# Interaction tower of 16 batches on one core: the last four batches' dense layers in groups of 2 and 2, and GpSimd makes part of batch 14's second products

## What is computed

```python
def _L0_rec_ref(x, Ws, bs):            # x (2048, 16, 256)
    xk = x
    outs = []
    for i in range(3):
        z = jnp.einsum('bfe,bge->bfge', x, xk).reshape(B_, F_ * F_, E_)
        z = jnp.swapaxes(z, 1, 2)
        z = jnp.einsum('bcl,oc->bol', z, Ws[i]) + bs[i][None, :, None]
        z = jax.nn.relu(z)
        z = jnp.sum(z, axis=-1)
        outs.append(z)
        xk = jnp.broadcast_to(z[:, :, None], (B_, F_, E_))
    return jnp.concatenate(outs, axis=1)
e = jnp.stack([tbl_0[ids[:, 0]], ..., tbl_15[ids[:, 15]]], axis=1)
z = _L0_rec_ref(e, L0_rec_Ws, L0_rec_bs)
h = jnp.concatenate([z.reshape(2048, -1), dense_ctx], axis=1)
h = jnp.maximum(h @ W_top1 + b_top1, 0.0)      # 64 -> 512
h = jnp.maximum(h @ W_top2 + b_top2, 0.0)      # 512 -> 256
y = h @ W_top3                                 # 256 -> 1
```

## Time and profile before

| | us |
|---|---|
| runs | 576.73, 579.08, 579.23 |
| median | 579.08 |
| the profiled execution | 579.74 |
| its span | 578.0 |
| last recorded instruction ends | 576.47 |

### The profile page before, as it was taken

How to read it: one execution, slowest core, us unless ns; L and a number is a source line. 1 busy time by engine, 2 the same in 40 slices (tenths; PEclk the granted TensorE clock), 3 DMA queues, 4 the chain that set the end, 5 groups by cost and what they waited for, 6 DMA issues and landing times.

```text
span 578.0 us, 10773 instructions
## 1 busy us (share of the span) xinstructions
PE 476.3 (82%) x3990; PEld 190.8 (33%) x3990; DVE 542.8 (94%) x326; ACT 498.7 (86%) x1471; POOL 467.8 (81%) x354
## 2 busy tenths in 40 slices
PE   5559888687888798878989788798869888789988
PEld 5213233232333333232333323233333323233324
DVE  1697999999999999999999999999999999999994
ACT  1143698999999999999999999989999999999875
POOL 6665888889888888888888889888888888888630
PEclk9689898999989989998999999799999989999979
DMA  3352212221222122212221222212212212210000
GB/s 98 92 145 74 75 56 57 63 64 56 74 58 64 56 71 72 67 56 74 62 64 56 69 60 61 73 57 82 64 56 66 61 60 74 57 54 1 1 2 0
DMA packets 14334, 35.43 MB, mean 61 GB/s; under 512 B 5493, under 2 KB 5879, under 8 KB 14266
## 3 DMA queue, kind: packets, MB, share of 16 engines
q0 software_dynamic: 12288, 33.57, 20.3%
q1 hardware_dynamic: 1994, 1.17, 0.8%
HBM read 34.71 MB, written 0.01 MB: 60 GB/s over the span
## 4 chain that ended last, share of the span: by engine, by line
DVE 38%; ACT 28%; PE 18%; issue 10%; POOL 3%; another core or an unknown queue 1%; DMA 1%; ACTq 0%; DVEq 0%; POOLq 0%
DVE prod L436 32%; ACT outer L637 15%; PE z_ps L827 8%; DVE outer L485 6%; ACT outer L627 3%; ACT sq L582 3%; POOL x_rows L342 3%; PE t_ps L790 3%; ACT relu L593 2%; ACT xt L574 2%; PE turn_ps L898 1%; PE turn_ps L902 1%; PE turn_ps L860 1%; PE zs_ps L842 1%
## 5 line engine op out<-in xcount | busy, mean ns | idle before, releaser
L436 DVE TENSOR_TENSOR prod<-t_ps,xt 128x2048 f32<-128x2048 f32 x190 | 420.8, 2281 | 11.0 <-remote 6.7
L342 POOL DMA_INDIRECT x_rows<-in_tbl,ids_sb x256 | 248.4, 970 | 73.1 <-issue 62.0
L637 ACT ACTIVATE outer<-outer,bias_sb 128x256 f32<-128x256 f32 x476 | 236.7, 518 | 3.0 <-DVE outer L485 3.0
L827 PE MATMUL z_ps<-prod,w_sb 128*32 128x512 f32 x1520 | 191.2, 622 | 37.3 <-DVE prod L436 34.3
L356 POOL TENSOR_TENSOR intra<-xt 128x1024 f32<-128x1024 f32 (+4 forms) x90 | 205.1, 2281 | 6.0 <-PE z_ps L827 4.5
L574 ACT ACTIVATE xt<-t_ps 128x512 f32<-128x512 f32 x128 | 75.2, 604 | 45.2 <-PE t_ps L790 21.7
L637 ACT ACTIVATION_READ_ACCUMULATOR outer<-outer,bias_sb 128x1 f32 x476 | 100.2, 210 | 0.0
L485 DVE TENSOR_TENSOR outer<-y_ps,z_all 128x1408 f32<-128x1408 f32 (+2 forms) x60 | 93.4, 1598 | 4.5 <-ACT outer L627 3.5
L790 PE MATMUL t_ps<-ident,x_rows 128*128 128x128 f32 x512 | 81.2, 288 | 19.0 <-DMA x_rows<-in_tbl,ids_sb 7.1
L827 PEld LDWEIGHTS z_ps<-prod,w_sb 128*32 128x32 f32 x1520 | 45.8, 111 | 124.8 <-issue 93.3
L790 PEld LDWEIGHTS t_ps<-ident,x_rows 128*128 128x128 f32 x512 | 55.9, 143 | 81.8 <-issue 59.6
(11 more groups left out here) (69 smaller groups left out, 219.1 us busy)
## 6 DMA issues: line engine op xcount, KB each, us to landing
x_rows<-in_tbl,ids_sb POOLq DMA_INDIRECT x256
w_sb<-in_w SPq DMA_DIRECT2D x1, 512.0 KB
feat<-in_dense SPq DMA_DIRECT2D x1, 128.0 KB
w_sb<-in_w SPq DMA_DIRECT2D x1, 128.0 KB
ids_sb<-in_ids SPq DMA_DIRECT2D x1, 120.0 KB
ident<-in_identity SPq DMA_DIRECT2D x1, 64.0 KB, 2.1
w_sb<-in_w0t SPq DMA_DIRECT2D x1, 64.0 KB
sel_sb<-in_sel SPq DMA_DIRECT2D x1, 48.0 KB
```

Of the source, the lines that this page charges most:

```text
L342: pool.indirect_dma_start(out=x_rows[:, par, f, :], out_offset=None, in_=tables[f], in_offset=bass.IndirectOffsetOnAxis(ap=ids_sb[:, NF * ...
L436: dve.tensor_tensor(prod[:, m % PROD_RING, half, :].rearrange("p (f g s) -> p f g s", f=QF, g=QF), t_ps[:, tbank(b, q, half), :, :].unsque ...
L637: act.activation(outer_of(b)[:, o // OP, o % OP, :], outer_of(b)[:, o // OP, o % OP, :], ACT.Relu, bias=bias12_sb[:, layer - 1, o:o + 1], ...
L827: mm = pe.matmul(z_ps[j * GR:(j + 1) * GR, m % 2, 0:n], w0_sb[:, half, slot, :], src[:, half, j * n:(j + 1) * n], start=(slot == 0 and hal ...
```

## The change

The dense groups of the tail become two and two batches (256 columns each). The first group's features, batches 12 and 13, are ready early, so TensorE runs its first layer directly behind z of layer 0 and the y step of group 2. For this the steps of group 2 move up: h2 step 0 goes to frame 14's slot `mlp_c`, h2 step 1 to frame 15's `mlp_a`, y to `mlp_b`. ScalarE's order in the tail changes with it, and batch 14's features are turned only behind the first dense group, directly ahead of batch 15's in TensorE's program; the 8 warming transposes stand ahead of both. `VECTOR_SUMS` gives VectorE 12 channels of batch 15's layer 1 and ScalarE 4. GpSimd makes channels 12 to 15 of batch 14's layer 2 (`outer_former`) from a new copy of y on ScalarE (`copy_y_former`), and VectorE's second piece shrinks from 8 channels to 4.

```diff
-LAST_TURN = ((0, "feat"), (0, "mlp_a"), (0, "yt"), (0, "mlp_b"), (1, "feat"), (0, "mlp_c"), (2, "feat"))
+LAST_TURN = ((0, "feat"), (0, "mlp_a"), (0, "yt"), (0, "mlp_b"), (1, "feat"), (2, "feat"))
...
-TAIL_GROUPS = (3, 1)
+TAIL_GROUPS = (2, 2)
...
-VECTOR_SUMS = {(2, 2): 4, (1, 1): 10, (1, 2): 8}
+VECTOR_SUMS = {(2, 2): 4, (1, 1): 12, (1, 2): 8}
...
         def mlp_slot(frame, kind):
...
+            if frame == LAST or (frame, kind) == (LAST - 1, "mlp_c"):
+                i = M1 + (frame - LAST + 1) * (1 + s)
+                return (t, i, range(M2 if i == M1 + M2 else M1)) if i <= M1 + M2 else None
...
+            def outer_former():
+
+                pool.wait_ge(y_copied, 1)
+                pool.wait_ge(z_ready, z_count(LAST - 1, 1))
+                o = NF - LAST_OP
+                y = y_former[:, :, :, :].rearrange("p f c o -> p o (f c)")
+                pool.tensor_tensor(
+                    outer[:, o // OP, o % OP:o % OP + LAST_OP, :].rearrange("p o (g f) -> p o g f", g=NF),
+                    y.unsqueeze(2).to_broadcast([P, LAST_OP, NF, NF]),
+                    z_all[:, (LAST - 1) % 2, 1, :].unsqueeze(1).unsqueeze(3).to_broadcast([P, LAST_OP, NF, NF]),
+                    ALU.mult).then_inc(pool_outer, 1)
...
-                n = op(b)
+                n = min(op(b), vector_channels(b, layer) - o)
...
+            def copy_y_former():
+
+                act.wait_ge(y_turned, LAST)
+                act.activation(y_former[:, :, :, :], y_ps[:, :, :, 1, NF - LAST_OP:NF], ACT.Copy).then_inc(y_copied, 1)
...
                 if i == 0:
-                    pe.wait_ge(turn_moved, turn(LAST + 1 + g, "feat") + 1)
+                    pe.wait_ge(turn_moved, turn(LAST + 2 * g, "feat") + 1)
+                if g == 0 and i == 2:
+                    pe.wait_ge(outer_done, piece(LAST - 1, 2, OP) + 1)
```

More of the change, by code:

```diff
@@ L37 @@
 FIRST_READ = (1, 0)
-WARM = {"first": 28, "second": 22, "end": 8}
+WARM = {"first": 28, "second": 22, "tail": 8}
 PROD_RING = 3
@@ L86, in build @@
         z_all = sb("z_all", [P, 2, NL, NF])
+        y_former = sb("y_former", [P, QF, GROUPS, LAST_OP])
         y_last = sb("y_last", [P, QF, GROUPS, 2, LAST_OP])
@@ L212, in op, with vector_channels @@
             return LAST_OP if b == LAST else OP
-        def vector_channels(b):
-            return NF - LAST_OP if b == LAST else NF
+        def vector_channels(b, layer):
+            return NF - LAST_OP if (b, layer) > (LAST - 1, 1) else NF
         def piece(b, layer, o):
-            return 2 * PIECES * b + vector_channels(b) // op(b) * (layer - 1) + o // op(b)
+            return 2 * PIECES * b + vector_channels(b, 1) // op(b) * (layer - 1) + o // op(b)
         def mlp_slot(frame, kind):
@@ L228, in mlp_slot @@
             if kind == "mlp_c":
-                done = t if frame == LAST else t - 1
-                return (done, M1 + M2, range(M2)) if done >= 0 and (at == 0 or frame == LAST) else None
+                return (t - 1, M1 + M2, range(M2)) if t > 0 and at == 0 else None
             if at < 2:
                 return t, 2 * at + s, range(1)
-            if frame == LAST:
-                return t, M1 + s, range(M1)
             return t, M1 + at - 2, range(M1 // 2 * s, M1 // 2 * (s + 1))
@@ L419, in _ @@
             multiply_last_unit(1)
+            outer_former()
             outer_last(1)
@@ L478, in outer_piece @@
                         dve.wait_ge(y_turned, b + 1)
-                        if b == LAST:
-                            dve.wait_ge(y_copied, 1)
+                        if b >= LAST - 1:
+                            dve.wait_ge(y_copied, b - LAST + 2)
                     if (b, layer) != (LAST, 1):
@@ L491, in outer_pieces @@
             def outer_pieces(b, layer):
-                for o in range(0, vector_channels(b), op(b)):
+                for o in range(0, vector_channels(b, layer), op(b)):
                     outer_piece(b, layer, o)
@@ L498, in vector_sum @@
                 for o in range(first, last):
-                    if o < vector_channels(b):
+                    if o < vector_channels(b, layer):
                         dve.wait_ge(outer_done, piece(b, layer, o) + 1)
                     else:
-                        dve.wait_ge(pool_outer, layer)
+                        dve.wait_ge(pool_outer, 1 if b < LAST else 1 + layer)
                     dve.scalar_tensor_tensor(
@@ L548, in _ @@
             outer_pieces(LAST, 1)
-            vector_sum(LAST, 1, 6, 16)
+            vector_sum(LAST, 1, 4, 16)
             outer_pieces(LAST, 2)
@@ L731, in _ @@
             copy_tile(LAST, 3, 1)
+            copy_y_former()
             move_z0(LAST - 1)
@@ L751, in _ @@
             sum_outer(LAST - 1, 2, 4, 8)
[L752 removed]
             mlp_in(LAST, "mlp_b")
[L754 to L757, removed]
+            sum_outer(LAST, 1, 0, 4)
             tail_move(0, 0)
@@ L761, in _ @@
             tail_move(0, 3)
-            mlp_in(LAST, "mlp_c")
-            sum_outer(LAST, 2, 0, 2)
-            sum_outer(LAST, 2, 2, 4)
+            sum_outer(LAST - 1, 2, 8, 12)
             tail_move(0, 4)
             tail_move(0, 5)
-            sum_outer(LAST, 2, 4, 6)
-            sum_outer(LAST, 2, 6, 8)
+            move_feat(LAST - 1)
+            sum_outer(LAST, 2, 0, 4)
+            sum_outer(LAST, 2, 4, 8)
             move_feat(LAST)
@@ L949, in keep_warm @@
             def keep_warm(when):
-                out = turn_ps[:, 0:P] if when == "end" else zs_ps[:, 0:P]
                 for _ in range(WARM[when]):
-                    pe.transpose(out, ident[:, :], ident[:, :])
+                    pe.transpose(turn_ps[:, 0:P] if when == "tail" else zs_ps[:, 0:P], ident[:, :], ident[:, :])
             pe.wait_ge(ident_loaded, 16)
@@ L1032, in _ @@
             tail_y(0)
-            pe.wait_ge(turn_moved, turn(LAST + 2, "feat"))
-            keep_warm("end")
+            pe.wait_ge(turn_moved, turn(LAST + 1, "feat"))
+            keep_warm("tail")
+            form_feat(LAST - 1)
             form_feat(LAST)
```

4 lines of the change are left out of this document (1 added, 3 removed).

## The result

| | before | with the change |
|---|---|---|
| median of 6 runs, us | 579.13 | 584.66 |
| lowest and highest | 576.73, 579.61 | 583.29, 586.58 |
| profiled execution | 579.74 | 585.32 |
| last recorded instruction ends | 576.47 | 581.66 |

The ratio is 1.0111, with a 95% interval of 1.0079 to 1.0143 (it isn't quite the ratio of the two medians); later runs of both kernels gave 1.0089 (1.0056 to 1.0121). The change makes the kernel slower by about 1%, 5.5 us by the medians. The forecast, 582.3, had the sign, the engines and the places, but only 3.2 us above the median before, and 2.6 above the profiled execution.

The account below looks back on a forecast made before the run. VectorE hardly rests in the loop; the end hangs on a chain from batch 15's layer 0 z through ScalarE's sums and TensorE's dense passes. Profiled 579.74 + 0.1 (full clock) + 2.5 (half clock) = 582.3 us, range 578.5 to 585.5.

Parts of the forecast that it names:

- forecast case: Whole change: parts 1 to 4 hold, last dense group starts at half clock; 581.0 to 583.5 us, chance 0.50.
- part 4: Last dense group: TensorE's clock falls in the 4.3 us gap before it, costing 2.5 us (1.65 to 3.25).
- part 3: Tail's new order: last features turned 3.0 us earlier, the 256-column last group takes 8.0 instead of 4.9.
- at full clock the change is worth +0.1: End of the tail before any clock loss: last move at 576.55 us against 576.47.
- Part 1: Frame 14: the added dense pass delays ScalarE's tile copy by 3.3 us and batch 15's layer 0 z by 2.5.
- Rival (C): Frame 14's slot hides the long pass, so everything from 544.89 on is 2.5 us earlier; chance 0.10.
- Part 2: Batch 14's second products: GpSimd takes four channels, saving VectorE 1.1 us, and 2.25 more on a long sum.
- rival (D): Batch 14's second products: GpSimd's product blocks VectorE's first piece, 2.3 us on the path, 584.6 us; chance 0.04.
- Rival (A): First dense group: a second low clock stretch on its second-layer matmuls costs 1.7 to 2.6 us, 584.4; chance 0.24.

Follow-up runs that it names:

- former_only: The kernel before with GpSimd's part alone (y copy, GpSimd's product of four channels, VectorE's second piece halved): 579.91 us, ratio 1.0010.
- warm_both: The changed kernel with batch 14's features turned directly behind the first dense group, 46 warming transposes after them, 9 and 3 ahead of z's fold: 581.0 us.
- before_again: The kernel before, unchanged, measured once more under its own label: ratio 1.0009.
- after_again: The changed kernel, unchanged, measured once more against the kernel before: ratio 1.0089.
- best31: The kernel before with 9 warming transposes ahead of batch 14's features, GpSimd's part, and ten VectorE sums of batch 15's layer 2, not eight: 578.69 us.
- steps_up: The kernel before with only group 2's dense steps moved a slot earlier, groups of 3 and 1 batches kept: 581.98 us.

## Why the prediction was right in kind and off in size

Every mechanism of the forecast case was there. What failed is the size, and no single term carries it: of the 3.0 us that were missing between the profiled executions, part 4's clock term was 0.8 too small (2.5 where 3.33 was measured, beyond its upper bound of 3.25), part 3's dense passes were taken at full clock and ran partly at half (0.6 with the rest of that sum), and two terms stood at nothing, the loop's arrival (1.1) and what passes behind the last move (0.4). The sentence "at full clock the change is worth +0.1" failed as well: with full clock on both sides it is +3.25, since the base of that sum had a low stretch in it.

By its own steps, in the profiled executions, counted from the landmark. The difference of 5.58 (585.32 - 579.74) is 2.66 to z, -4.86 from z to the features, 6.27 from there to the last move, 0.39 outside of these, and 1.12 of the loop's arrival.

**Part 1 was right.** 2.5 forecast, 2.66 measured, 2.62 by leaving the pass out. ScalarE's copy of the tile came 3.4 later against the landmark, 3.3 forecast, and its rest of 2.59 ahead of the move is the mechanism as described. Frame 13's short pass was a fair sign that the slot's cover is short. Rival (C) is out.

**Part 2 was right.** A piece half as long, no long sum, and no block of VectorE by GpSimd (3.42 for its two pieces with GpSimd beside it), so rival (D) is out. The Trainium skill (SBUF — State Buffer, Who interferes with whom) has it so for a VectorE instruction with one input in SBUF; the trace agrees again. VectorE's first products of batch 15 stood 0.26 earlier against the landmark, 0.4 forecast. former_only shows what this is worth by itself: nothing that can be told from the noise (1.0010, 0.9980 to 1.0040).

**Part 3's order was right, its base was wrong.** I priced the new middle with TensorE at full clock and set it against a profile of before whose w3 pass had run at half clock. So I expected the way from z to the features to shrink by 5.5 (the 3.0 gained in all and the 2.5 that part 1 had cost before it), and it shrank by 4.86. The new w3 pass was low, too, and ScalarE waited 1.04 for it, which cost 0.4 at the features; the rest of the 0.6 is the sum's own error. More telling is like with like: with full clock in both, the tails are 61.75 (warm_both, which has the other order and the warming, too) and 58.50 (before_again), a loss of 3.25 and not of 0.1. The middle gives 2.3, the last group costs 2.9, the pass 2.6. The 3.0 "gained" at the last features was the base's low stretch, 3.3 us.

**Part 4 had the mechanism and undersized the term.** TensorE's gap was forecast at 4.3 and was 4.34. 2.5 was taken between 1.65 and 3.25; 3.33 was measured (10.87 - 7.54), just beyond the upper bound, and 4.1 in after_again (11.62 - 7.54). The doubled width was sized rightly: 2.94 at full clock (7.54 - 4.60), some 3.1 forecast. The upper bound was read from the longest low stretch of the tail of before (6.5). after_again had one from 573.3 to 583.5, nearly the whole group. The Trainium skill (TensorE: Matmul & The Clock Gate, What's actually happening) calls the throttled clock the default, which activity lifts; the windows agree, with 0.14 busy in 4.40 ahead of the fall.

**Rival (A)** came to pass beside the forecast case and not in its stead, at a lower price than 1.7 to 2.6. In the first profile of the change the low stretch fell on the w3 pass and cost 0.4 (16.49 against 16.06). In after_again it fell on the second-layer matmuls, where I had put it, and cost some 1.0.

**Not foreseen:** 0.39 between the last move and the reported time, 3.66 against 3.27, in the changed kernel and its kin. best31 has it too, steps_up and former_only don't; no run tells what makes it. The loop's 1.1 is scatter by the arrivals. Against the profiled execution the sum was 2.6 and 5.6 came. Of the 3.0 between them, 0.7 belongs to the last group (0.8 of clock less 0.1 of width), 0.6 to part 3, 0.2 to part 1, 0.4 lies outside and 1.1 is the loop. The 5.5 between the medians is another matter: the tail of the change with its 0.4 stands 4.5 above the one tail of the kernel before (61.81) and 7.7 above the other (58.50), and 5.5 lies between. That the medians mix the two is an estimate from these; no run tells how often each tail comes.

## What to carry to other kernels

Fit the clock's state into the base before comparing: a sum that takes its new passes at full clock has to take the old ones at full clock as well, or it books the base's bad luck as a gain. Where reordering opens a rest of TensorE ahead of a serial stretch of matmuls, fill it up to the instruction that ends it, and not from the point at which it begins. And a step that is moved off the last stretch has to land where the engines that wait for it have a rest; here it landed in front of a tile that ScalarE and VectorE were about to need.

## What the runs showed that I had not expected

Warming that stops early was worth nothing: after 3.9 us of gapless transposes TensorE was busy for 0.27 in 1.70, the clock fell at 571.0, and the last group was as long as without them (10.87 in both). Second, once low, the clock was low through all of the last group's first-layer steps, although TensorE was busy throughout (571.11 to 574.76 in the changed kernel, 575.15 to 578.93 in after_again), and rose only during the second-layer matmuls (at 578.1 and 583.5); with the later rise the group took 11.62 and not 10.87. Third, a program's part that nobody touched reached its end over 6 us apart in different profiles (512.87 to 519.24), which is more than the whole effect that was to be measured.
